# Rows of the sequence two ahead scaled ahead of the selection, and the zero fill issued from two queues

## What is computed

```python
x = L0_attn_x                                             # 8 x 256 x 256
x = x + L0_attn(layernorm(x))                             # decaying linear attention, 16 heads of 16
x = x + L0_ffn(layernorm(x))                              # 64 experts, top 8 of each row, capacity 512
x = x + L1_attn(layernorm(x))                             # decaying linear attention, 16 heads of 128, gated
x = x + L1_ffn(layernorm(x))                              # dense gated feed-forward, 1024 wide

# L0_ffn: every row goes to its 8 best experts, in the order of the rows
probs = softmax(x @ gate_w.T); scores, idx = top_k(probs, 8)
pos = place of the pair among those of the same expert; valid = pos < 512
xbuf = zeros((64, 512, 256)).at[expert, pos].set(row, mode='drop')
y = (silu(xbuf @ w_gate) * (xbuf @ w_up)) @ w_down
out = zeros.at[row].add(y[expert, pos] * score * valid)
```

## Time and profile before

| | us |
|---|---|
| median of 3 runs | 1481.93 |
| lowest and highest | 1480.17, 1482.09 |
| profiled execution, its own time | 1483.07 |
| profiled execution, span from first to last instruction | 1481.4 |
| TensorE's mean granted clock, share of full | 0.943 |
| busy share of the span: PE, DVE, ACT, POOL | 87%, 68%, 54%, 30% |

### The profile page before, as it was taken

The page is one execution under the profiler, slowest core; times in us unless marked ns, Lnnn a source line. Parts: engine busy times, 40 slices in busy tenths (PEclk is TensorE's granted clock), DMA queues, the critical chain, the costliest instruction groups (busy, mean ns, idle before and its releaser), DMA issues.

```text
span 1481.4 us, 28437 instructions
## 1 busy us (share of the span) xinstructions
PE 1286.6 (87%) x9120; PEld 1143.1 (77%) x9120; DVE 1000.5 (68%) x2071; ACT 798.9 (54%) x1543; POOL 449.8 (30%) x490
## 2 busy tenths in 40 slices
PE   4657666069999999957999999999999999999996
PEld 4434444058888888846989989999899899998996
DVE  5565657437777777755767767677677676776665
ACT  4211221236666666634666666666666666666663
POOL 1045556711111111142523325225233262251010
PEclk9988888579999999978999999999999999999998
DMA  9992122258989989850101001001010010010000
GB/s 312 424 337 75 65 75 95 92 168 296 305 289 304 291 300 305 295 191 22 40 15 33 19 15 51 1 25 39 14 32 18 14 50 0 28 36 1 8 1 8
DMA packets 58382, 173.65 MB, mean 117 GB/s; under 512 B 10064, under 2 KB 26960, under 8 KB 56144
## 3 DMA queue, kind: packets, MB, share of 16 engines
q1 hardware_dynamic: 35952, 103.61, 19.8%
q0 software_dynamic: 21504, 67.13, 14.4%
q10 hardware_dynamic: 864, 2.12, 0.4%
HBM read 86.83 MB, written 85.98 MB: 117 GB/s over the span
## 4 chain that ended last, share of the span: by engine, by line
PE 63%; DVE 12%; DMA 12%; issue 6%; ACT 4%; SPq 2%; POOL 1%; DVEq 0%; ACTq 0%; POOLq 0%
PE bank L787 17%; DMA experts<-in_moe_in 9%; PE bank L792 8%; PE bank L839 6%; PE bank L776 6%; PE bank L822 4%; PE bank L812 4%; PE bank L880 3%; PE bank L823 2%; PE bank L813 2%; PE bank L609 1%; DVE experts L1489 1%; DVE experts L1502 1%; ACT experts_r L957 1%; DVE W L1313 1%
## 5 line engine op out<-in xcount | busy, mean ns | idle before, releaser
L787 PE MATMUL bank<-layer_r 128*128 128x256 f32 x2048 | 309.0, 288 | 11.0 <-issue 4.9
L1293 DVE TENSOR_TENSOR layer_r<-W,layer_r 128x1024 fp32r<-128x1024 f32 (+2 forms) x229 | 256.3, 1120 | 50.1 <-ACT layer_r L1113 50.1
L787 PEld LDWEIGHTS bank<-layer_r 128*128 128x128 f32 x2048 | 267.2, 191 | 15.9 <-issue 12.8
L1113 ACT ACTIVATE layer_r<-W 128x1024 fp32r<-128x1024 f32 (+2 forms) x226 | 221.7, 981 | 59.1 <-PE bank L839 37.2
L525 POOL TENSOR_TENSOR layer<-layer 128x256 f32<-128x256 f32 x120 | 87.4, 729 | 422.9 <-ACT layer L1188 422.4
L708 PE MATMUL bank<-experts_r 128*96 128x512 f32 x768 | 195.4, 404 | 4.8 <-DVE experts_r L1477 4.5
L495 POOL DMA_INDIRECT rows<-y_rows,sidx x128 | 169.8, 1327 | 55.2 <-issue 31.7
L792 PE MATMUL bank<-layer_r 128*128 128x256 f32 x1024 | 175.6, 284 | 0.0
L708 PEld LDWEIGHTS bank<-experts_r 128*96 128x96 f32 x768 | 121.9, 164 | 53.6 <-issue 8.0
L426 POOL DMA_INDIRECT y_rows<-W x128 | 126.5, 988 | 95.6 <-issue 58.0
L792 PEld LDWEIGHTS bank<-layer_r 128*128 128x128 f32 x1024 | 146.0, 192 | 0.0
(11 more groups left out here) (141 smaller groups left out, 2263.7 us busy)
## 6 DMA issues: line engine op xcount, KB each, us to landing
y_rows<-D SPq DMA_DIRECT2D x32, 1024.0 KB, 38.8
experts<-y_rows POOLq DMA_DIRECT2D x64, 512.0 KB, 4.4
y_rows<-experts SPq DMA_DIRECT2D x64, 512.0 KB, 4.3
W<-in_w SPq DMA_DIRECT2D x32, 416.0 KB, 5.1
experts<-in_moe_in SPq DMA_DIRECT2D x64, 192.0 KB, 4.7
experts<-in_moe_down SPq DMA_DIRECT2D x64, 96.0 KB, 4.3
y_rows<-W POOLq DMA_INDIRECT x128, 2.4
rows<-y_rows,sidx POOLq DMA_INDIRECT x128, 3.2
```

The source lines that it names most:

```text
L787: pe.matmul(out, Whi1[s][:, c * step + at:c * step + at + P], x_[:, c, :], start=(n == 0 and c == 0 and x_ is hi), stop=False, skip_group_ ...
L1113: nc.scalar.activation(Whi1[i % 2][:, 0:W.shape[1]], W, ACT.Copy).then_inc(S["d_whi"], 1)
L1293: return nc.vector.tensor_tensor(dst, src, hi.bitcast(F32), ALU.subtract)
```

## The change

Two edits, independent of each other in the code. On VectorE, `a_norm(b + 2)` is moved from behind the five steps of the selection to ahead of them, behind `a_stats(2)` of turn 0. In the zero fill, SyncE keeps the transfers of even j (lower 64 partitions, 8 of the low and 8 of the high half); GpSimd issues those of odd j: 8 of the low half ahead of the second of its first three powers, 8 of the high half ahead of the third, each with semaphores of their own. Who waited for a half now waits for both of its semaphores.

```diff
         NSMALL = 5
+        pieces = y_rows.rearrange("(e h j n) d -> h j e (n d)", h=2, j=ROW_FILLS // 2, n=H1 * SEQ // D)
+
+        def zeros(half):
+            return D1[E * half:E * (half + 1)].rearrange("p a b -> p (a b)")
...
             sp.wait_ge(S["zeros_ready"], 1)
-            n = H1 * SEQ // D
-            pieces = y_rows.rearrange("(e h j n) d -> h j e (n d)", h=2, j=ROW_FILLS // 2, n=n)
             for h, done in enumerate(("low_rows_cleared", "high_rows_cleared")):
-                for j in range(ROW_FILLS // 2):
-                    zeros = D1[E * (j % 2):E * (j % 2 + 1)].rearrange("p a b -> p (a b)")
-                    sp.dma_start(pieces[h, j], zeros).then_inc(S[done], 16)
+                for j in range(0, ROW_FILLS // 2, 2):
+                    sp.dma_start(pieces[h, j], zeros(0)).then_inc(S[done], 16)
...
             for i, (lo, hi) in enumerate(STATS):
+                if i == 1:
+                    pool.wait_ge(S["zeros_ready"], 1)
+                    for j in range(1, ROW_FILLS // 2, 2):
+                        pool.dma_start(pieces[0, j], zeros(1)).then_inc(S["low_rows_cleared2"], 16)
+                if i == 2:
+                    for j in range(1, ROW_FILLS // 2, 2):
+                        pool.dma_start(pieces[1, j], zeros(1)).then_inc(S["high_rows_cleared2"], 16)
                 rsqrt(pool, "a_var", "a_rstd", varA[:, lo * TB:hi * TB], rstdA[:, lo * TB:hi * TB], i + 1)
...
                     if b == 2:
-                        pool.wait_ge(S["low_rows_cleared"], 16 * (ROW_FILLS // 2))
+                        pool.wait_ge(S["low_rows_cleared"], 16 * (ROW_FILLS // 4))
+                        pool.wait_ge(S["low_rows_cleared2"], 16 * (ROW_FILLS // 4))
                     if b == 3:
-                        pool.wait_ge(S["high_rows_cleared"], 16 * (ROW_FILLS // 2))
+                        pool.wait_ge(S["high_rows_cleared"], 16 * (ROW_FILLS // 4))
+                        pool.wait_ge(S["high_rows_cleared2"], 16 * (ROW_FILLS // 4))
...
                 if b == 0:
                     a_stats(2)
+                if b + 2 < NB:
+                    a_norm(b + 2)
                 if back:
                     a_select(b - 1)
                     a_places(b - 1)
                     a_slots1(b - 1)
                     a_slots2(b - 1)
                     a_slots3(b - 1)
-                if b + 2 < NB:
-                    a_norm(b + 2)
```

More of the change, by code:

```diff
@@ L271, in build @@
         a_out_ps a_x1 a_xh2 a_x2T_ps a_x2T a_log_ps a_logit a_ln_steps a_var a_rstd a_ln2_steps a_var2 a_rstd2
-        a_sel_steps a_ntop a_exp a_selb a_rank_ps a_pos_steps a_slot_steps a_scat zeros_ready low_rows_cleared high_rows_cleared
+        a_sel_steps a_ntop a_exp a_selb a_rank_ps a_pos_steps a_slot_steps a_scat zeros_ready low_rows_cleared high_rows_cleared low_rows_cleared2 high_rows_cleared2
         b_x_ps b_xhi b_xlo b_whi b_wlo b_dhi b_dlo
@@ L1044, in _ @@
                 turn(b, b < NB, b + 1 < NB, b > 0)
-            act.wait_ge(S["high_rows_cleared"], 16 * (ROW_FILLS // 2))
+            act.wait_ge(S["high_rows_cleared"], 16 * (ROW_FILLS // 4))
+            act.wait_ge(S["high_rows_cleared2"], 16 * (ROW_FILLS // 4))
             decay(1, D1, "decay1_exp", range(H1))
```

## The result

The changed kernel takes 1473.36 us at the median (1470.65 to 1477.89, 6 runs) against 1481.96 of before: a ratio of 0.9948, 95% interval 0.9928 to 0.9969. That is 8.6 us faster where 30.75 were forecast, and outside the stated range of 1446 to 1462.

The account below looks back on a forecast made before the run. Layer 0's turns were taken as bound by a loop through a_norm; -30.75 (turns) - 1.0 (clock) + 1.0 (start) + 0 (fill) + 0 (issues) = -30.75 gave a median of 1451.2 us, range 1446 to 1454.

Parts of the forecast that it names:

- What bounds the stage: Layer 0: each turn's length is set by a loop of transposes, TensorE's work, selection of the sequence before and a_norm.
- The reordering, -30.75: Layer 0, turns 1 to 5: a_norm ahead of the selection starts the next transposes 6.15 us earlier, five times.
- VectorE's and GpSimd's margins: Within a turn: VectorE free at 9.9 us against 10.74; GpSimd's a_norm2 ending near 14.6, third mask at 16.04.
- The clock, -1.0: TensorE in layer 0: shorter gaps may keep clock 1.00 in some turns; at most 0.8 us a turn, 1.0 taken.
- GpSimd's issues, 0: GpSimd's zero transfers ahead of its second and third powers: 0.54 us an issue, no loss up to 1.9 us each.
- The rival in which GpSimd stalls on issuing: GpSimd's queue takes new zeros only as old ones land: 1498 us; chance 0.05 slower, 0.03 a stall in part.
- The start, +1.0: Loads at the kernel's start, beside a second stream of zeros from 6.3 us: 1.0 us lost, bounds 0 and 2.
- the 3.7 us of cover behind the second power: GpSimd's second power, at 17.65 us, could come 3.7 us later without loss.
- The fill, 0: Divided zero fill: ends at 100 to 107 us, scatter of sequence 1 at most 2.7 us late, no loss.
- no sooner: Rival on the zero fill: it ends as before, 3.9 us lost in turn 3, 1455.1 us; chance 0.21.
- the rival with one half alone: Zero fill: SyncE's queue served first, GpSimd's rest read from one half at 265 GB/s, 1452 to 1462 us; chance 0.09.
- the 2.7 us of margin: Turn 3, behind the scatter of sequence 1: slack around the third mask that absorbs 2.7 us of a late fill.

Follow-up runs that it names:

- e3: The reordering with the undivided fill on SyncE's queue, against the kernel before, every zero transfer reading partitions 32 to 95: 1447.69 us, ratio 0.9769.
- e1: The kernel before with the reordering alone, the whole zero fill on SyncE's queue with alternating halves: 1453.54 us, ratio 0.9817.
- e4: The changed kernel with both queues reading their zeros from partitions 32 to 95: 1449.28 us, ratio 0.9778 against the kernel before.
- e6: The changed kernel with each queue alternating between the halves instead of keeping one: 1488.38 us at the median of 10 runs, ratio 1.0039 against the kernel before.
- e9: The reordering with the fill on SyncE's queue alone, against the kernel before, halves changed after every eight transfers instead of every one: 1522.21 us, one run.
- e5: The changed kernel with GpSimd issuing its first zeros only when SyncE's last load has landed: 1474.26 us, ratio 0.9949 against the kernel before.
- e7: The kernel before, SyncE's queue alone, with every zero read from partitions 0 to 63: 1544.91 us, one run.
- e2: The kernel before with the division of the fill alone, a_norm left behind the selection: 1491.65 us, ratio 1.006.
- e10: The kernel before with its zeros read from partitions 32 to 95 and nothing else changed: 1482.41 us, ratio 0.9998.

## Why the prediction was wrong, point by point

- **What bounds the stage: right.** The loop through `a_norm` was the turn's length; with `a_norm` moved, `a_places` is what the transposes follow. One reading of it was loose: in the earlier trace rows slices 1 to 7 stand at 4 to 7 tenths, slice 8 at none and slice 10 at nine, so the first seven carry the argument.
- **The reordering, -30.75: right.** Four turns measured 24.3 to 24.6 against 24.4 forecast. Where the fill is out of the way (e3) the five turns save 153.05 - 119.95 = 33.1 us, clock included. VectorE's and GpSimd's margins held where the fill was out of the way. In the changed kernel they did not all hold: in turn 2 the first scatter waited for the low half, `a_norm2` started 16.3 us into the turn, where it was to end at 14.6, and the third mask began 0.9 us behind its forecast 16.04; the slack behind it took that up.
- **The clock, -1.0: right in kind, elsewhere than forecast.** In e3 the turns whose transposes began at a granted clock of 1.00 (four of them in 0.63 us; at 0.50 they take 1.09) took 23.4 and 23.5 us, the others 24.3 to 24.4; two of five were such, 1.8 us in all, 0.9 a turn where the cap was 0.8. In the changed kernel turns 1, 2, 4 and 5 all began at 0.50 or near it (transposes of 1.09 to 1.12 us) and gained nothing. The long turn and the last start began at 1.00, and behind the last start 1.2 us were gained (see the open end), which the forecast did not count.
- **GpSimd's issues, 0: right.** Eight took 4.41 us, 0.55 each, as its 0.54 us load suggested, and not SyncE's 1.63. The rival in which GpSimd stalls on issuing falls with that.
- **The start, +1.0: 0.2.** The residual load landed 4 us later (16.9 against 13.0 us to landing), and the 3.7 us of cover behind the second power took that; the first transposes of the loop moved from 49.25 to 49.47. e1 and e3, with the fill undivided, have them at 49.56 and 49.55, so the 0.2 are not told from the spread.
- **The fill, 0: the step that failed.** The estimate was an end at 100 to 107 us, the bound "no sooner" 110.5, and the rival with one half alone 108 to 118. It ended at 131.4, and the scatter was 28 us later than the 104.8 of the forecast; less the 2.7 us of margin that is 25.3, and the third turn shows 26.0. Three readings were wrong, and a fourth, wrong too, did no harm. First, was read as 32 transfers that start slowly and could start fast; the 265 GB/s were collisions within one half (a third of the packets slow from 10 to 30 us, none with partitions 32 to 95), but the 426 were not a property of the transfers, they were that of their order in one queue. Second, "both halves are read from the start" counted on both queues starting together; SyncE's zeros stood behind its loads, whose small packets now shared the DMA engines with 16 KB packets of GpSimd's (from 20 to 25 us, 63 packets of 64 B beside 62 of 16 KB): the last load took 27.8 us to land instead of 12.4. Third, the full DMA share was taken as a sign that nothing could be slower; it is full at 205 GB/s too. Fourth, the fifth of the share that was busy from 110 to 111 us was read as a tail of the fill; by the packet records it was the first scatter's rows, and the last zeros had ended at 109.9.
- **The rivals.** "One half ends alone" named the mechanism, at 0.09, but with the wrong queue in front (SyncE's, where it was GpSimd's) and without the loss in the middle: at 383 instead of 426 GB/s, and at half rate from 20 to 27 us. "No sooner" was tested by the kernel with the reordering alone: 1453.5 against 1455.1. The closeness is partly luck, since turn 3 lost 6.1 us there and not 3.9, and two turns at full clock gave 1.8 back.
- **The rule on two queues.** The Trainium skill (DMA: Bandwidth & Descriptors, Rules for kernel authors) says that spreading transfers over SP, ACT and GpSimd does not help the bandwidth, and of two transfers to disjoint halves not to bother. With partitions 32 to 95 e4 agrees with the first: the fill ends at 99.3 us with two queues, at 99.9 with one. With the halves the division cost 21 us, which neither the rule nor the forecast had.
- **Open.** Behind the last start the changed kernel is 3.7 us shorter. 1.2 us lie in turns 6 to 8 up to the last scatter (74.4 us from the last start, before 75.7). They go with the clock: in the four traces whose last start has a granted clock of 1.00 and takes its transposes in 0.63 us (changed kernel, e4, e6, e9) that stretch is 74.3 to 74.4 us, in the others 75.2 to 76.1. The other 2.4 lie in the experts and layer 1, which the change doesn't touch; that part takes 1200.5 to 1204.2 us over the twelve traces, with e5 at 1204.2 and the changed kernel at 1201.0, which is more than the 2.4 without any difference in the code there. What makes the collisions die out in one queue and not in two stays open.

## What to carry to other kernels

When a loop is shortened, a transfer that was just in time can become its bound; so before that, look up in the trace when each transfer that the loop waits for ends, and ask what the new order does to that end. A full DMA share says nothing of the rate: read the GB/s beside it, and the length of equal packets. 64 partitions were read at full rate by one queue and by two when no two of them lay 32 apart in one half (32 to 95), and at half or three quarters of it when all or half of them did (0 to 63, 16 to 79); the reordering with that one-line change takes 1447.69 us, 25.7 less than the changed kernel.

## What was not expected of the hardware

- A 16 KB packet out of SBUF takes 0.61 us with partitions 32 to 95 (e3) and 1.27 with 0 to 63 (e7), where each partition has another 32 further in its half that is read too; the whole rate is 203 to 211 GB/s then (e7, 20 to 80 us), against 416 to 442 (e3).
- Collisions can last: in e9 96% of the 16 KB packets that started from 20 to 130 us were slow, although the half changed twice in that time.
- The kernels with two queues whose zeros can collide vary more: e6 spread over 39 us in 10 runs and e2 over 9.3 in 4, against 1.3 in 4 for e4 and 5.2 in 10 for e10. Why was not shown.
- A 64 KB load and an 8 KB load behind each other in SyncE's queue took 19.3 and 27.8 us to land beside GpSimd's zeros (18.9 and 22.6 in e4, without collisions), 13.2 and 12.4 before.
